# A graph layer on one core: the first group's indices loaded by themselves, the keys with their neighbours in one pass, and two groups of edges before the block selection

## The reference, cut to what matters

```python
em = concat([x[src], x[dst]], -1)                       # per edge
em = relu(layer_norm(em @ msg_w + msg_b, msg_g, msg_beta)) * edge_weights[:, None]
messages = segment_sum(em, dst) / (counts + 1e-08) * (counts > 0)
gate = sigmoid(x @ gate_w + gate_b)                     # per node
h_new = relu(layer_norm(concat([x, messages], -1) @ upd_w + upd_b, upd_g, upd_beta))
out = layernorm(x + gate * h_new + (1 - gate) * x)
```

## Time and profile before

| | |
|---|---|
| time, median of 3 | 607.79 us (606.64 to 609.39) |
| profiled execution: its own time | 610.86 us |
| its span (first to last instruction) | 608.7 us |
| mean granted TensorE clock | 0.977 |
| busy share PE / DVE / ACT / POOL | 90 / 86 / 88 / 62% |
| `params_ready` (end of L946) | about 16.2 us |
| last matmul of group 1 (L761) ends | about 53.8 us |

### The profile page before, as it was taken

How to read it: one execution, slowest core, us unless ns; L and a number is a source line. 1 busy time by engine, 2 the same in 40 slices (tenths; PEclk the granted TensorE clock), 3 DMA queues, 4 the chain that set the end, 5 groups by cost and what they waited for, 6 DMA issues and landing times.

```text
span 608.7 us, 19214 instructions
## 1 busy us (share of the span) xinstructions
PE 546.4 (90%) x4552; PEld 522.7 (86%) x4600; DVE 525.0 (86%) x2406; ACT 534.5 (88%) x2504; POOL 379.1 (62%) x396
## 2 busy tenths in 40 slices
PE   1455999999999999999999999999999999999761
PEld 0445899899999999989999999999999999999661
DVE  6751389898999999989999999999999999999986
ACT  0223799999999999999999999999999999999883
POOL 2777777777777777777767677676776767200000
PEclk9986899999999999999999999999999999999996
DMA  4323678788888788787877878778787787756642
GB/s 101 97 71 107 168 186 222 205 209 217 213 212 226 196 224 217 209 222 194 226 217 205 228 192 220 211 210 225 187 228 213 205 226 193 204 157 169 166 118 69
DMA packets 193111, 115.12 MB, mean 189 GB/s; under 512 B 15085, under 2 KB 186550, under 8 KB 193078
## 3 DMA queue, kind: packets, MB, share of 16 engines
q1 hardware_dynamic: 178480, 87.95, 51.9%
q0 software_dynamic: 12544, 25.72, 18.6%
q10 hardware_dynamic: 2054, 1.08, 0.8%
HBM read 75.72 MB, written 38.97 MB: 188 GB/s over the span
## 4 chain that ended last, share of the span: by engine, by line
ACT 46%; PE 31%; issue 12%; DVE 5%; DMA 2%; SPq 2%; ACTq 1%; DVEq 0%
ACT squares L565 12%; ACT un L598 11%; ACT squares L539 6%; PE ps_u L779 5%; PE ps_u L781 5%; PE ps_z L761 3%; ACT xT L560 3%; PE ps_z L746 3%; ACT xdT L534 3%; PE ps_z L748 3%; PE ps_t L796 2%; ACT hT L611 2%; ACT emT L554 2%; PE ps_h L803 2%; PE ps_x L769 2%
## 5 line engine op out<-in xcount | busy, mean ns | idle before, releaser
L473 POOL DMA_INDIRECT pair_rows<-in_x,gather_idx x392 | 378.9, 967 | 143.2 <-issue 112.6
L779 PE MATMUL ps_u<-u_x_gate,xT 128*128 128x129 f32 x784 | 155.3, 280 | 11.0 <-ACT un L598 9.0
L781 PE MATMUL ps_u<-window,onehot 128*128 128x128 f32 x784 | 151.2, 274 | 0.0
L779 PEld LDWEIGHTS ps_u<-u_x_gate,xT 128*128 128x128 f32 x784 | 118.5, 191 | 14.8 <-issue 7.4
L781 PEld LDWEIGHTS ps_u<-window,onehot 128*128 128x128 f32 x784 | 119.0, 192 | 0.0
L598 ACT ACTIVATE un<-ps_u,u_rstd 128x128 f32<-128x128 f32 x392 | 112.4, 374 | 3.2
L1117 DVE TENSOR_SCALAR out_rows<-y,y_small,y_rstd 128x128 f32<-128x128 f32 x392 | 110.2, 357 | 4.5 <-ACT y_rstd L621 4.5
L565 ACT ACTIVATE squares<-ps_u 128x128 f32<-128x128 f32 x392 | 108.1, 302 | 4.9 <-PE ps_u L781 4.7
L1065 DVE SCALAR_TENSOR_TENSOR y<-ps_h,gate_small,x_rows 128x128 f32<-128x128 f32 x392 | 109.8, 342 | 1.1 <-PE ps_h L803 1.1
L565 ACT ACTIVATION_READ_ACCUMULATOR squares<-ps_u 128x1 f32 x392 | 90.4, 233 | 0.0
L1072 DVE BATCH_NORM_STATS2 y_stats<-y 128x6 f32<-128x128 f32 x392 | 84.7, 279 | 0.0
(11 more groups left out here) (132 smaller groups left out, 989.8 us busy)
## 6 DMA issues: line engine op xcount, KB each, us to landing
x_rows<-in_x SPq DMA_DIRECT2D x98, 256.0 KB
out<-out_rows SPq DMA_DIRECT2D x98, 256.0 KB
window<-rows_scratch SPq DMA_DIRECT2D x196, 112.9 KB
rows_scratch<-msg_rows SPq DMA_DIRECT2D x49, 258.0 KB
pair_rows<-in_x,gather_idx POOLq DMA_INDIRECT x392
const_in<-in_constants ACTq DMA_DIRECT2D x1, 570.0 KB, 7.2
rows_scratch<-pad_rows SPq DMA_DIRECT2D x5, 64.5 KB, 3.7
const_in<-in_constants SPq DMA_DIRECT2D x1, 320.0 KB, 3.8
```

The costliest lines, as they stand in the source:

```text
L473: return nc.gpsimd.indirect_dma_start(rows[:, j * P:(j + 1) * P], None, x, bass.IndirectOffsetOnAxis(ap=offsets, axis=0))
L779: nc.tensor.matmul(u_tile(j, ROW), tile(xT[b], j), u_x_gate[:], start=True, stop=False, skip_group_check=True)
L781: last = nc.tensor.matmul(u_tile(j, P), tile(onehot[b], j), window[slot][:, j * ROW:j * ROW + P], start=False, stop=True, skip_group_check ...
```

## The change

1. `first_indices`: SP and ACT each begin with a DMA of the first group's 512 indices, straight into the shape that the gather wants (`first_idx`, 128 x 4 words, one word to a descriptor). GpSimd waits for these two, gathers group 0 by them, and waits for `gather_idx` only ahead of group 1.
2. `spread_with_halo`: `halo_i` is filled with tiles and their neighbours in one pass of four DMAs from ACT, whose rows are 146 words long and overlap in DRAM: tiles 1 to 127, tiles 128 to 194, tile 0, the last tile. The nine DMAs of L355 and `next_i` go. `keys_loaded` now waits for all of it; `halo` is cast in one instruction; `first_next` comes from `halo`. The wait for `edges_loaded` moves to just ahead of `mean_weight`, and the weights' DMAs follow the source indices on SP directly.
3. TensorE takes the messages of group 0 ahead of the block selection, which is cut in two halves of 16 instructions; all of group 1, its transposes back and its update too, comes ahead of the branch. VectorE and ScalarE follow.

```diff
+        def first_indices(eng, v, side):
+            with nc.allow_non_contiguous_dma(reason="a word for each edge of a group"):
+                eng.dma_start(first_idx[:, side * T:(side + 1) * T],
+                              v[0:BN].rearrange("(t p) -> p t", p=P)).then_inc(first_loaded, 16)
+        def spread_with_halo(eng, v, buffer, semaphore):
+            full, over = ET - P - 1, E - (ET - 1) * P
+            wide = P + 2 * REACH
+            def tiles_from(t, n):
+                return bass.AP(v.tensor, v.offset + t * P - REACH, [[P, n], [1, wide]])
+            eng.dma_start(buffer[1:P, 0, :], tiles_from(1, P - 1)).then_inc(semaphore, 16)
+            eng.dma_start(buffer[0:full, 1, :], tiles_from(P, full)).then_inc(semaphore, 16)
+            eng.dma_start(buffer[0:1, 0, REACH:], row(v, 0, P + REACH)).then_inc(semaphore, 16)
+            eng.dma_start(buffer[full:full + 1, 1, 0:REACH + over], row(v, (ET - 1) * P - REACH, REACH + over)).then_inc(
+                semaphore, 16)
         def _(sp):
+            first_indices(sp, src, 0)
             sp.dma_start(ident, consts[:, C_IDENT:C_IDENT + P]).then_inc(ident_loaded, 16)
             sp.wait_ge(pads_ready, 1)
             spread(sp, src, src_i, keys_loaded)
-            sp.wait_ge(pads_ready, 4)
-                for a, b in ((next_i[:, 0:1], after[0:P, 0:1]),
...
-                    sp.dma_start(a, b).then_inc(edges_loaded, 16)
+            sp.wait_ge(pads_ready, 3)
             spread(sp, edge_weight, weight_f, edges_loaded)
...
+                        indices = first_idx[:, j:j + 1] if g == 0 else gather_idx[:, g, j:j + 1]
...
+            pool.wait_ge(first_loaded, 32)
+            gather(0)
             pool.wait_ge(idx_ready, 2)
-            for g in range(SLOTS):
+            for g in range(1, SLOTS):
                 gather(g)
...
+            first_indices(act, dst, 1)
+            act.wait_ge(pads_ready, 2)
+            spread_with_halo(act, dst, halo_i, keys_loaded)
...
-            pe.wait_ge(params_ready, 1)
-            def mean_weights():
+            def first_half():
+                block_selection(range(T))
+            def other_half():
                 table_transposes(3, mean_weight, ps_u[:, 256:512])
+                block_selection(range(T, 2 * T))
...
-            head((mean_weights, general_and_starts))
+            pe.wait_ge(params_ready, 1)
+            head((first_half, other_half, general_and_starts))
             with is_general(pe):
-                rest_of_head()
...
-            dve.wait_ge(keys_loaded, 16 * 6)
+            dve.wait_ge(keys_loaded, 16 * 7)
             v.tensor_copy(src_f[:], src_i[:]).then_inc(table_in, 1)
-            link(v.tensor_copy(here, halo_i[:, :, REACH:REACH + P]))
+            link(v.tensor_copy(halo[:], halo_i[:]))
...
-            dve.wait_ge(edges_loaded, 16 * 12)
-            v.tensor_copy(first_next[:], next_i[:])
+            v.tensor_copy(first_next[:], halo[:, :, REACH + P:REACH + P + 1].rearrange("p c a -> p (c a)"))
...
-            v.tensor_copy(halo[:, :, 0:REACH], halo_i[:, :, 0:REACH])
-            link(v.tensor_copy(halo[:, :, REACH + P:], halo_i[:, :, REACH + P:]))
...
+            dve.wait_ge(edges_loaded, 16 * 3)
             v.tensor_tensor(mean_weight[:], weight_f[:], recip[:], ALU.mult).then_inc(table_in, 1)
...
-                dve.wait_ge(sel_done, 1)
+            def block_starts():
+                dve.wait_ge(sel_done, 2)
                 for n in range(2 * T):
                     last = v.tensor_scalar(fine_out[:, n], sel_out(n)[:, 0:P],
```

More of the change, by code:

```diff
@@ L335, in _ @@
         def _(sp):
-            full = ET - P - 1
-            by_tile = dst[0:(ET - 1) * P].rearrange("(t q) -> t q", q=P)
-            before = dst[P - REACH:P - REACH + (ET - 2) * P].rearrange("(t q) -> t q", q=P)[:, 0:REACH]
-            after = dst[P:(ET - 1) * P].rearrange("(t q) -> t q", q=P)[:, 0:REACH]
+            first_indices(sp, src, 0)
             sp.dma_start(ident, consts[:, C_IDENT:C_IDENT + P]).then_inc(ident_loaded, 16)
@@ L343, in _ @@
             spread(sp, src, src_i, keys_loaded)
-            sp.wait_ge(pads_ready, 4)
-            with nc.allow_non_contiguous_dma(reason="a word for each tile"):
-                for a, b in ((next_i[:, 0:1], after[0:P, 0:1]),
-                             (next_i[0:full - 1, 1:2], after[P:, 0:1]),
-                             (next_i[full - 1:full, 1:2], row(dst, (ET - 1) * P, 1)),
-                             (halo_i[1:P, 0, 0:REACH], before[0:P - 1]),
-                             (halo_i[0:full, 1, 0:REACH], before[P - 1:]),
-                             (halo_i[full:full + 1, 1, 0:REACH], row(dst, (ET - 1) * P - REACH, REACH)),
-                             (halo_i[:, 0, REACH + P:], after[0:P]),
-                             (halo_i[0:full - 1, 1, REACH + P:], after[P:]),
-                             (halo_i[full - 1:full, 1, REACH + P:], row(dst, (ET - 1) * P, REACH))):
-                    sp.dma_start(a, b).then_inc(edges_loaded, 16)
+            sp.wait_ge(pads_ready, 3)
             spread(sp, edge_weight, weight_f, edges_loaded)
@@ L509, in _ @@
         def _(act):
+            first_indices(act, dst, 1)
+            act.wait_ge(pads_ready, 2)
+            spread_with_halo(act, dst, halo_i, keys_loaded)
             with nc.allow_non_contiguous_dma(reason="vectors of 128 as columns"):
-                act.wait_ge(pads_ready, 2)
-                spread(act, dst, halo_i[:, :, REACH:REACH + P], keys_loaded)
                 act.dma_start(weights[:, 0:2], msg_w.rearrange("(a k) h -> k a h", a=2)).then_inc(weights_loaded, 16)
@@ L628, in to_rstd @@
                 z_rstd_of(g)
-            def whole_edge(g):
-                to_rstd(g)
                 emT_of(g)
             def head():
-                whole_edge(Step(0))
-                to_rstd(Step(1))
+                for g in range(HEAD):
+                    whole_edge(Step(g))
             def step(at):
@@ L702, in _, with block_selection @@
                 table_transposes(i, table, ps)
-            pe.wait_ge(sel_ready, 1)
-            for n in range(2 * T):
-                for c in range(2):
-                    last = nc.tensor.matmul(sel_out(n), sel[:, c, n * P:(n + 1) * P], sel_rhs[:, c, :],
-                                            start=c == 0, stop=c == 1)
-            last.then_inc(sel_done, 1)
-            pe.wait_ge(params_ready, 1)
-            def mean_weights():
+            def block_selection(tiles_of_block):
+                pe.wait_ge(sel_ready, 1)
+                for n in tiles_of_block:
+                    for c in range(2):
+                        last = nc.tensor.matmul(sel_out(n), sel[:, c, n * P:(n + 1) * P], sel_rhs[:, c, :],
+                                                start=c == 0, stop=c == 1)
+                last.then_inc(sel_done, 1)
+            def first_half():
+                block_selection(range(T))
+            def other_half():
                 table_transposes(3, mean_weight, ps_u[:, 256:512])
+                block_selection(range(T, 2 * T))
             def general_and_starts():
@@ L1129, in head @@
                 rows(Step(0))
-                for task in between[1:]:
+                for task in between[1:2]:
                     task()
                 z_norm(Step(1))
+                for task in between[2:3]:
+                    task()
             def step(at):
```

37 lines of the change are left out of this document (16 added, 21 removed).

## The result

The changed kernel takes 613.03 us (median of 5 runs, 611.67 to 614.96), the kernel before 607.79 (606.64 to 609.39, 5 runs): ratio 1.0087, 95% interval 1.0064 to 1.0109. It is slower, where 606.2 was forecast, and outside the range of 601.0 to 610.7. The profiled execution took 612.56 (span 610.7), against 610.86 (608.7) for that of before. What I read from the two traces therefore bears on the sign and the mechanism; the size comes from the medians.

What follows compares the result with a forecast made beforehand. The start-up before the loop was taken as what the change moves. Gain 8.5 us behind the parameters, less 5.9 for late keys and 1.0 for the clock, made 1.6: 607.79 to 606.2 us, own range 601.5 to 610.5, 8-in-10 range 601.0 to 610.7.

Steps and rivals of the forecast that it cites:

- R: The end of the parameters, at 16.22 us in the kernel before, from which the forecast counts the later stages.
- the hand-over: Start of group 2's transposes, 53.84 us before; taken as the moment the change can move.
- First gap: TensorE idle between group 1's update and group 2's transposes, forecast at 3 to 3.5 us because of the branch.
- chain behind R: Stages from the parameters' end to group 2's transposes: 37.6 us before, forecast 29.1, a gain of 8.5.
- D: Delay of the parameters' end by late keys, forecast 5.9 us, within 3 to 9.
- second wait for instructions: Another TensorE instruction wait behind the branch, among group 2's transposes; the forecast priced only the branch.
- clock: TensorE's lower clock around group 2's message, booked as a loss of 1.0 us, between -1 and +3.
- the first wait: TensorE's branch to a far target waits for its instructions, forecast at 3.8 us ahead of group 2's transposes.
- Rows 5: Profile rows of ACT's queue before, 23 packets from 6.0 to 6.5 us, read as one stream at 22 ns each.
- The index loads: Two loads of the first group's indices ahead of the keys, 1,024 descriptors, booked at 1.0 us of delay.
- My slow rival: ACT's queue backs up behind the keys, biases land late, parameters' end 9.7 us later: 611.3 us, chance 0.14.
- The two fast rivals: Keys hardly late, 0.5 to 2 us: 601.5, chance 0.26; branch covered, no hole: 601.7, chance 0.10.

Runs made afterwards that it cites:

- e1: The changed kernel with the long key loads in DMAs of 112, 15, 64 and 3 rows instead of 127 and 67: 608.05 us, ratio 0.998.
- e3: The changed kernel without the bodies for general edges, a drain in their place, so TensorE's jump is short: 610.05 us, ratio 0.9992.
- e7: The changed kernel with its wide keys undone, so narrow keys and nine small loads; index loads and new order stay: 608.47 us, ratio 1.0009.
- e5: The kernel before with only the wide keys of the change's second part, in DMAs of 127, 67, 1 and 1 rows: 614.78 us, ratio 1.007.
- e11: The changed kernel with all long loads divided and without the bodies for general edges: 601.52 us, ratio 0.9894.
- e6: The kernel before with only the wide keys, their rows divided into 112, 15, 64 and 3: 610.62 us, ratio 1.0039.
- e10: The changed kernel with the branch's flag computed early and its keys left in 127 and 67 rows: 609.95 us, ratio 0.9989.
- e8: The kernel before without the bodies for general edges, a drain in their place: 607.73 us, ratio 0.9964.
- e9: The changed kernel with all long loads divided and the branch's flag computed early: 606.19 us, ratio 0.9942.

## Why the prediction was wrong, step by step

Seen from R, the hand-over stands at 52.39 - 23.89 = 28.5 us, and was forecast at 29.1. `zn` of group 0: R + 9.8 (forecast 10.1 to 10.8). `zn` of group 1: R + 21.3 (22.1). Update 1 ends at R + 25.3 (25.6). First gap 3.22 us (3.5), branch 3835 ns (3.8). The chain behind R, which took most of the working, was right within 1 us at each of these links. What failed, in gains:

| term | forecast | trace after |
|---|---|---|
| chain behind R | +8.5 | 37.6 - 28.5 = +9.1 |
| delay D of R | -5.9 | -7.7 |
| second wait for instructions | not seen | -2.6 |
| clock | -1.0 | -2.1 |
| sum at `zn` of group 2 | +1.6 | -3.3 |

The last line is the trace's 63.73 - 60.45; the clock's term is what remains when the others are taken off. The sum's own range was added up a little too narrow: D from 3 to 9 and the clock from +1 to -3 give 601.3 to 611.3, where 601.5 to 610.5 was written; 613.03 lies outside either. The runs then differ by 5.2 us (3.9 to 6.6 by the interval).

**"The hand-over", taken as the point behind which nothing changes, is the step that failed.** "That moment is what the change can move": I followed the branch to its target and stopped there. Group 2's second set of transposes waits once more, 2.64 us, for the next packet of instructions. Two packets can be read in before's trace (in the windows 45.5 to 46.5 and 49.5 to 50.5); I priced one wait alone. e1, e3 and e7 show the pair (2.54, none and 2.21 us for the second gap), and e3 shows that with a short jump neither exists. The Trainium skill, "Runtime: NRT & Kernel Launch", section "Instruction fetch mechanics", on which I leaned, was right about the first wait (3835 ns with the far target, 223 without), and e3 bears out its rule that the far target makes it; the second wait had to be read from the DMA rows. The same section calls the passage from one block of instructions to the next mostly hidden; behind this jump the trace disagrees, with 2.64 us exposed.

**D was mis-sized, with the right mechanism.** I took 5.9 from a single stream at 22 ns a row; R moved by 7.7, the keys by 7.1. e1 moved the keys back to 8.40 by nothing but the row counts, and e5 made them late by nothing but part 2: it is how 127 and 67 rows are shared out. The Trainium skill, "DMA: Bandwidth & Descriptors", section "Why a DMA increments its semaphore by 16 and not by 1", says that a DMA goes over the largest number of engines up to 16 that divides its outer size. The runs agree: 127 rows (one engine by that rule) 15.01, 112 + 15 rows 8.40, and from 6 to 7 us in the change both queues together fill 7.3% of the time of 16 engines. Rows 5 were a poor place to read the price: their 23 packets took 24.7% of 16 engines' time, which is four engines and not one. In the change a row took 28 ns, so the 194 rows come to 5.4 us, where I had booked 4.3 + 0.6 = 4.9; and e5, which has no index loads, moved the cast by 6.6. The index loads, booked at 1.0, cost about 0.5 by e5, which is within the scatter of the traces. About 1.1 us of the stream's price stays unexplained. The other 0.6 us of D is the wait for the biases (0.89 instead of 0.47) and small steps behind it.

My slow rival had a piece of this right: ScalarE's queue was held up by the loads of the keys, issued the last bias load 4.8 us later (9.07 against 4.24), and the biases did come last. But they were awaited for 0.89 us and not for 6.3, and D was 7.7 where the rival needed 9.2. That it named nearly the right time (611.3) was luck: the second gap, which it did not have, made up for its missing delay.

**The clock** was booked at -1.0 with a bound of 2.3 if group 2's message runs low. It did, and 2.1 is what remains for it. I had tied the lower clock to the hole ahead of group 2, and that was not shown to be its cause: in the change it had fallen before the gap, and in e3, without a gap, group 2's message ran low as well, and the stretch behind group 1's update was 1.6 us longer than before. So the gaps alone do not decide it: e3 without them is low, e1 with them is low too, and e11, without them and with early keys, has group 2's message at full clock (0.39 us for two instructions). What does decide it stays open.

**The size beyond the head.** At `zn` 2 the change was 3.3 us late, at the end of the profiled spans 2.0, and by the medians 5.2. I have no trace that explains the difference between 3.3, 2.0 and 5.2; over all thirteen kernels the rest of the span scatters by 4 us (546.0 to 549.9) without any order that I can see, so it stays open.

The two fast rivals fall: the keys were late, and the branch was not covered.

## What to carry to other kernels

Count a DMA's rows before making it wider: merging small loads into one with 127 rows cost more (5.1 us alone, e5) than the nine loads it removed. Cutting the long loads into 112 + 15 and 64 + 3 gave back 6.5 us in the change (by the ratios, e1), and about half of the cost in the kernel before (e6). A far branch costs in each place where the sequencer next runs out of instructions, so follow the instruction queue's packets behind the target, and lay all of them under a wait that TensorE has in any case. Book the lower clock for a stage by itself, with the stage's rows at either level: here it came with and without a hole in front of the stage (after, e3), and took back up to 2 us of a better order.

## What the runs showed of the hardware

- The far jump on TensorE took 3.4 to 5.6 us in the branch itself (3375 ns in e7, 5569 in e10), and a short one 223 to 231 ns (e3, e11, e8). GpSimd's took 45 ns in every run, with its own general body or without.
- The second wait behind the jump, 2.2 to 2.6 us (e7, e1, after), comes after only four transposes; in the change one packet of 16 KB on the instruction queue goes with each wait.
- Loads of 127 and 67 rows, of 584 and 512 bytes, went as one stream for both plain queues: 36 packets from 6 to 7 us in the change, 7.3% of the time of 16 engines.
- The lower clock outlasts the holes: after, it was at 0.50 from 48 to 60 us, though TensorE worked in three stretches of that. It does not need them: without a wait for instructions between group 1's update and group 2's message, that message ran mostly low in e3 (two instructions in 0.63 us) and at full clock in e9 and e11 (0.39 us; in e9 the mean of 46 to 48 us was 0.63 already).
- Two runs of the same kernel can differ by more than the whole effect of this change (before: 605.65 to 613.76 over the chips). One profiled span told the sign here, and would have told it wrong for e6 and e8.
